# Searching the next batch's bound inside the present batch, and making keys and one-hots during the router

## The reference, cut to what matters

```python
sim = einsum('bhnd,bhmd->bnm', Q, K) / (sqrt(d) * H)     # 4 x 512 x 512
k = int(n * 0.3)                                         # 153
threshold = top_k(sim, k)[0][:, :, -1:]
A = sigmoid(sim) * (sim >= threshold)
A = (A + swapaxes(A, -1, -2)) * 0.5
x = x + (1 - gamma) * layernorm(x) + gamma * A
h = layernorm(x)
scores = sigmoid(h @ router_w)                           # 4 of 8 groups, then 8 of 32 experts
routed = sum over the 8 experts of weight * (silu(h @ w_gate) * (h @ w_up)) @ w_down
shared = silu(h @ sw_gate) * (h @ sw_up) @ sw_down
x = x + routed + shared
```

## Time and profile before

| | us |
|---|---|
| three executions | 1115.98, 1116.62, 1118.31 |
| median | 1116.62 |
| the profiled execution, its own time | 1117.09 |
| its span (first to last instruction) | 1115.4 |

### The profile page before, as it was taken

How to read it: one execution, slowest core, us unless ns; L and a number is a source line. 1 busy time by engine, 2 the same in 40 slices (tenths; PEclk the granted TensorE clock), 3 DMA queues, 4 the chain that set the end, 5 groups by cost and what they waited for, 6 DMA issues and landing times.

```text
span 1115.4 us, 21197 instructions
## 1 busy us (share of the span) xinstructions
PE 925.1 (83%) x4604; PEld 485.6 (44%) x4605; DVE 586.5 (53%) x1362; ACT 457.3 (41%) x894; POOL 514.2 (46%) x396
## 2 busy tenths in 40 slices
PE   3367775775776799999999999999999999999985
PEld 1143342442432355555445555555454454545542
DVE  5959859768555444344644444444544545454321
ACT  5253243241312244345544444454454545454331
POOL 2026126145154055555554555555456463566543
PEclk8568787887887899999999999999999999999998
DMA  5111030110232567777887777778777788786654
GB/s 178 56 39 50 1 119 7 38 41 1 76 116 83 187 130 170 173 169 166 229 179 179 159 166 185 178 156 179 193 181 168 220 181 248 160 179 112 122 108 72
DMA packets 90269, 149.26 MB, mean 134 GB/s; under 512 B 9648, under 2 KB 46768, under 8 KB 90224
## 3 DMA queue, kind: packets, MB, share of 16 engines
q0 software_dynamic: 33120, 80.64, 37.1%
q1 hardware_dynamic: 57104, 68.13, 18.5%
HBM read 101.55 MB, written 47.20 MB: 133 GB/s over the span
## 4 chain that ended last, share of the span: by engine, by line
PE 47%; issue 8%; DVE 3%; DMA 3%; ACT 3%; DVEq 2%; ACTq 2%; POOL 2%; SPq 0%; POOLq 0%
PE bank L254 40%; PE bank L1396 4%; PE bank L1387 3%; DMA stage_dn<-in_L_ffn_w_down_dram 3%; ACT gu L236 2%; DVEq L1069 2%; ACTq L1069 1%; DVE gu L243 1%; POOL mark_q L408 1%; DVE hid L1303 1%; DVE dn L246 0%; POOL mark_q L405 0%; DVE hT L1312 0%; DVEq L243 0%; ACT silu L1164 0%
## 5 line engine op out<-in xcount | busy, mean ns | idle before, releaser
L254 PE MATMUL bank<-gu,xgT 128*128 x1764 | 408.5, 382 | 13.6 <-issue 9.3
L1115 POOL DMA_INDIRECT out_dram<-y,ids_i x145 | 242.0, 1669 | 286.8 <-DMA out_dram<-y,ids_i 152.7
L254 PEld LDWEIGHTS bank<-gu,xgT 128*128 128x128 f16 x1764 | 173.1, 98 | 196.2 <-issue 25.7
L254 PE MATMUL bank<-dn,hT 128*128 x870 | 212.0, 380 | 15.6 <-issue 15.6
L1103 POOL DMA_INDIRECT xg<-xrows,ids_i x153 | 158.3, 1034 | 75.2 <-issue 40.8
L1303 DVE SCALAR_TENSOR_TENSOR hid<-bank,xg,silu 128x256 f32<-128x256 f32 x146 | 70.4, 482 | 207.3 <-ACT silu L1164 180.3
L1176 ACT CAST hT<-bank 128x256 f16<-128x256 f32 x146 | 53.7, 368 | 226.7 <-PE bank L1387 213.7
L1312 DVE TENSOR_TENSOR hT<-bank,hT 128x256 f16<-128x256 f32 x146 | 61.8, 423 | 153.0 <-ACT hT L1176 147.0
L1183 ACT ACTIVATE y<-bank 128x512 f32<-128x512 f32 x145 | 86.6, 597 | 133.4 <-PE bank L254 124.4
L254 PEld LDWEIGHTS bank<-dn,hT 128*128 128x128 f16 x870 | 84.9, 98 | 90.3 <-issue 23.0
L254 PE MATMUL bank<-xT,gu 128*128 128x512 f16 x384 | 98.0, 421 | 25.4 <-DVE hid L303 25.4
(11 more groups left out here) (210 smaller groups left out, 803.6 us busy)
## 6 DMA issues: line engine op xcount, KB each, us to landing
stage_gu<-in_L_ffn_w_gate_dram SPq DMA_DIRECT2D x32, 512.0 KB
stage_gu<-in_L_ffn_w_up_dram SPq DMA_DIRECT2D x32, 512.0 KB
stage_dn<-in_L_ffn_w_down_dram SPq DMA_DIRECT2D x32, 512.0 KB
x_sb<-in_x_dram SPq DMA_DIRECT2D x4, 1024.0 KB, 6.2
xrows<-adj SPq DMA_DIRECT2D x4, 1024.0 KB, 4.1
out_dram<-acc SPq DMA_DIRECT2D x4, 1024.0 KB, 4.4
xg<-xrows,ids_i POOLq DMA_INDIRECT x153
out_dram<-y,ids_i POOLq DMA_INDIRECT x145
```

Source lines behind the costliest of these rows:

```text
L254: last = nc.tensor.matmul(out_ap, stationary(a, c), moving(w, c), start=(c == 0 and (a, w) == parts[0]), stop=(c == chunks - 1 and (a, w) ...
L1115: g_.indirect_dma_start(out, bass.IndirectOffsetOnAxis(ap=ids_i[:, t:t + 1], axis=0), y[:, t % YS, :], None, compute_op=ALU.add).then_inc( ...
```

## The change

The search of batch b + 1 no longer stands at the head of batch b + 1. `search` is cut into `search_step` and `bound`. Batch 0 has its five steps ahead of the loop, as before with two tiles on each engine. For the later batches VectorE counts one tile and ScalarE three, and the steps stand in the batch before: the first guess between the aggregates and the normalising, step 0 after the normalised rows, step 1 after the one-hots, step 2 in the middle of `routing`, steps 3 and 4 behind it. Keys and `mark_slots` of batch p stand ahead of step 1; `mark_parts` is split: the subtraction stays on GpSimd (`part_parts`, after the low parts of the rows), and the comparison goes to VectorE, between steps 3 and 4. The moments of `sim` come from ScalarE: the sum from the copy out of PSUM, the sum of squares from a Square pass. There are two roots a batch for one. All four products of the shared expert stand in `bound` and `update`. `rank_tokens` comes a batch later on TensorE, `sum_marks` after the gate-and-up pieces 0 and 1, `turn_found` a further step on. The down products use banks 7, 5, 6, 7. In the second block the last batch's keys and first product have moved to the end of the first block, and pieces are interleaved in another order.

```diff
-        TB, SIMB, MISC, DB = (0, 1), (2, 3), 4, 7
+        TB, SIMB, MISC = (0, 1), (2, 3), 4
+        DB = (7, 5, 6, 7)
...
+        RANKB = (MISC,) * (B - 1) + (SIMB[0],)
...
         def s_down(pe, b, i):
             pe.wait_ge(S["s_lo"], SC * (b + 1))
-            if b or i:
-                pe.wait_ge(S["added"], RT * b + i)
+            if i == RT - 1:
+                pe.wait_ge(S["added"], RT * b + 1)
...
+        def mark_parts(dve, b, g):
+            n = RT * b + g
+            dve.wait_ge(S["parts_apart"], n + 1)
+            nc.vector.tensor_scalar(mark_q[:, g, :, :], mark_q[:, g, :, :], 0.0, row_idf[:, n:n + 1], ALU.is_equal, ALU.mult).then_inc(S["marks_q_ready"], 1)
...
@@ GpSimd, a batch
-                        pool.wait_ge(S["keys_ready"], b)
-                        for half in range(2):
-                            for g in range(2 * half, 2 * half + 2):
-                                mark_parts(pool, b - 1, g)
-                            s_low(pool, b - 1, 2 * half)
-                            s_low(pool, b - 1, 2 * half + 1)
+                        for c in range(SC):
+                            s_low(pool, b - 1, c)
...
+                    if b >= 1:
+                        pool.wait_ge(S["keys_ready"], b)
+                        for g in range(RT):
+                            part_parts(pool, b - 1, g)
@@ TensorE, a batch
                     if p >= 0:
                         s_gate_up(pe, p, 2)
+                    if p >= 1:
+                        turn_found(pe, p - 1)
...
                     adjacency_T(b)
+                    if p >= 0:
+                        rank_tokens(pe, p)
                     if b + 1 < B:
                         similarities(b + 1)
                     if p >= 0:
                         s_down(pe, p, 1)
-                        sum_marks(pe, p)
                         s_down(pe, p, 2)
-                        turn_found(pe, p)
                     rows_T(b)
...
                     s_gate_up(pe, b, 0)
-                    s_gate_up(pe, b, 1)
-                    rank_tokens(pe, b)
+                    if b + 1 < B:
+                        s_gate_up(pe, b, 1)
+                        if p >= 0:
+                            sum_marks(pe, p)
+                    else:
+                        sum_marks(pe, p)
+                        s_gate_up(pe, b, 1, (0,))
+                        rank_tokens(pe, b)
+                        s_gate_up(pe, b, 1, (1,))
+                        turn_found(pe, p)
@@ ScalarE, a batch
+                    if p >= 0:
+                        s_high(act, p, 0)
+                        s_high(act, p, 1)
+                        s_silu(act, p, 2)
...
                     if more:
                         similarities(b + 1)
+                        squares(b + 1)
+                        nth += 1
+                        root(nth, slice(1, 3))
+                        counts(b + 1, 0, first)
+                    nth += 1
+                    root(nth, slice(0, 1))
+                    if more:
+                        counts(b + 1, 0, second)
+                        counts(b + 1, 1, first)
+                    for i in range(RT):
+                        transposed_rows(b, i)
+                    if more:
+                        counts(b + 1, 1, second)
+                        counts(b + 1, 2, first)
                     act.wait_ge(S["logits_ready"], b + 1)
...
+                        counts(b + 1, 2, second)
                         sigmoids(b + 1)
+                        if p < 0:
+                            convert_high(act, 1)
+                        counts(b + 1, 3, range(1, RT))
                         s_silu(act, b, 0)
+                        counts(b + 1, 4, range(1, RT))
+                        s_silu(act, b, 1)
@@ VectorE, a batch
+                    bound(b)
...
+                    nth = update(b, nth)
+                    if more:
+                        search_step(b + 1, 0)
                         coefficients(b + 1)
+                    if p >= 0:
+                        s_add(dve, p, 2)
+                        find_keys(dve, ch, p)
+                        s_add(dve, p, 3)
+                        for g in range(RT):
+                            mark_slots(dve, p, g)
+                        if not more:
+                            for g in range(RT):
+                                mark_parts(dve, p, g)
+                    if more:
+                        search_step(b + 1, 1)
                     routing(b)
+                    if more:
+                        search_step(b + 1, 3)
+                        if p >= 0:
+                            for g in range(RT):
+                                mark_parts(dve, p, g)
+                        else:
+                            convert_low(dve, 1)
+                        search_step(b + 1, 4)
+                    else:
+                        s_product(dve, b, 0)
+                        find_keys(dve, ch, b)
```

More of the change, by code:

```diff
@@ L692, in similarities, with squares, counts, transposed_rows @@
                         act.wait_ge(S["sim_ready"], RT * b + i + 1)
[L693 removed]
+                        if b == 0:
+                            nc.scalar.mul(sim[:, i, :], bank[SIMB[i % 2]][:, :], SIM_SCALE).then_inc(S["sim_copied"], 1)
+                        else:
+                            nc.scalar.activation(sim[:, i, :], bank[SIMB[i % 2]][:, :], ACT.Identity, scale=SIM_SCALE,
+                                                 accum_out=s_sum[:, i:i + 1]).then_inc(S["sim_copied"], 1)
+                def squares(b):
+                    act.wait_ge(S["act_counted"], counted(b - 1, STEPS - 1))
+                    for i in range(RT):
+                        act.wait_ge(S["sim_copied"], RT * b + i + 1)
+                        nc.scalar.activation(junk[:, i, :], sim[:, i, :], ACT.Square, accum_out=s_sq[:, i:i + 1]).then_inc(S["squares_ready"], 1)
+                def counts(b, k, tiles):
+                    act.wait_ge(S["mid_ready"], b * (STEPS + 1) + k + 1)
+                    if b >= 1:
+                        act.wait_ge(S["squares_ready"], RT * b)
+                    for i in tiles:
+                        nc.scalar.activation(junk[:, i, :], sim[:, i, :], ACT.Sign, bias=mid[:, i:i + 1], scale=-1.0,
+                                             accum_out=act_cnt[:, i:i + 1]).then_inc(S["act_counted"], 1)
+                def transposed_rows(b, i):
+                    act.wait_ge(S["xnT_ready"], RT * b + i + 1)
+                    act.wait_ge(S["xn_ready"], b + 1)
+                    nc.scalar.copy(xT32[:, i, :, :], bank[TB[i % 2]][:, :].rearrange("p (k t) -> p k t", k=KC)).then_inc(S["xT32_ready"], 1)
+                    nc.scalar.copy(xT16[:, 0, :, columns(b, i)],
+                                   bank[TB[i % 2]][:, :].rearrange("p (k t) -> p k t", k=KC)).then_inc(S["xhi_ready"], 1)
                 def sigmoids(b):
@@ new lines, in search_step @@
+                def search_step(b, k):
+                    tiles = DVE_TILES if b == 0 else 1
+                    own, acts = slice(0, tiles), slice(tiles, RT)
+                    dve.wait_ge(S["mid_ready"], b * (STEPS + 1) + k + 1)
+                    if b >= 1:
+                        dve.wait_ge(S["squares_ready"], RT * b)
+                    for i in range(tiles):
+                        ch.done(v.tensor_scalar(junk[:, i, :], sim[:, i, :], mid[:, i:i + 1], 0.0, ALU.is_ge, ALU.add,
+                                                accum_out=cnt[:, i:i + 1]))
+                    ch.settle()
+                    ch.done(v.scalar_tensor_tensor(dlt[:, own], cnt[:, own], -WANTED, slope[:, own], ALU.add, ALU.mult))
+                    dve.wait_ge(S["act_counted"], counted(b, k))
+                    ch.step(v.scalar_tensor_tensor(dlt[:, acts], act_cnt[:, acts], 2 * WANTED - N, slope[:, acts], ALU.add, ALU.mult))
+                    v.scalar_tensor_tensor(mid[:, :], dlt[:, :], DAMPING[k], mid[:, :], ALU.mult, ALU.add).then_inc(S["mid_ready"], 1)
```

254 lines of the change are left out of this document (118 added, 136 removed).

## The result

The kernel before took 1116.3 us (median of four executions, 1115.94 to 1118.31), the changed one 1104.36 us (1102.87 to 1107.48): a ratio of 0.9893, 95% interval 0.9868 to 0.9918. The forecast was 1101.5 in 1094 to 1110. The profiled execution took 1105.09 us with a span of 1103.0; forecast for the span 1100.3. One execution of all those reported here, of the changed kernel with one bank, took 1423.2 us at a granted clock of 0.64 where the others of it had 0.93, and it is in no ratio and no median.

The account below looks back on a forecast made before the run. VectorE, with TensorE close behind, was taken to bound the 369 us before the tile stage. The last addition 15.1 us earlier gave span 1115.4 - 15.1 = 1100.3, predicted time 1101.5 us, range 1094 to 1110.

Parts of the forecast that it names:

- X of batch 1: Start of the four last counts (L852) in batch 1: claimed at 94.3 us, 14.4 earlier than before.
- X to Y: From four last counts to first addition of the transposed adjacency: 30.2 us for 18.1; last batch 29.3 for 18.0.
- Y to T: First addition of the transposed adjacency to end of normalised rows: 16.0 us for 16.6; last batch 12.8 for 16.4.
- R to X: Start of routing to the four last counts, middle batches: 12.9 us for 29.0, 16.1 won.
- T to R: End of normalised rows to start of routing: 18.6 us for 11.9; last batch 14.0 for 9.9.
- Keys end at 318.0: End of the last batch's keys: 318.0 us for 319.55, leaving 1.5 us of the 14.4 won earlier.
- From there 36.1 to the last addition: Last batch's keys to end of the last addition before the tiles: ending at 354.1 us, 15.1 earlier than 369.2.
- (a): Sign is not in the root's table, so more table loads round the second root: +3.8 us, 1105; chance 0.12.
- (b): TensorE's gate-up 2 behind the four last counts is granted 2.4 GHz: 8 us less, 1093.5; chance 0.11.
- (d): TensorE stays at 1.2 GHz through the whole chain of the front: 20 us more, 1121.5; chance 0.07.
- (c): First tile waits for expert weights or rows, so half of the 13.6 us is lost: 1108; chance 0.11.
- (e): The search misses its eight candidates and falls back to 26 bisections: above 1200 us; chance 0.01.

## Why the prediction was right, and where it was off

The forecast, 1101.5 us and faster, held: 1104.36. By its own steps:

- *X of batch 1 at 94.3*: 93.24. *X of batch 2 at 172.0, of batch 3 at 250.0*: 172.39 and 250.99. The forecast had batches 1 and 2 give back 5.0 of the 14.4 us that batch 0 wins, and the last batch most of the rest; batches 1 and 2 gave back 7.0 of 15.5, and the last batch the other 8.5 and 1.5 more. That the two marks came so close is partly luck: a batch is 79.15 and 78.60 long for 77.7 and some 78, but X of batch 1 was 1.1 early.
- *X to Y 30.2, then 29.3 without mixing*: 30.0, 29.5, 28.75. The reason given, TensorE's chain behind product 0, is shown by the runs with the products moved: without it X to Y is 19.6 to 21.4.
- *Y to T 16.0 and 12.8*: 15.2, 15.2 and 12.6. A Square pass took 0.62 for the 0.71 it was priced at. *R to X 12.9*: 12.8 twice.
- *T to R 18.6, and 14.0 in the last batch*: 21.1, 21.1 and 16.3. This is the main term that was mis-sized, by its contention between VectorE and GpSimd. The one-hots were taken at 5.2 with GpSimd beside them and took 6.92, 6.96 and 7.43; step 1 behind them was taken at 1.25 and took 2.1, beside GpSimd's next instructions. That is the 2.5. The bound given for the one-hots, 4.6 to 6.5, was passed, though the forecast had itself put GpSimd beside them, and the earlier trace rows has two of them at 3.23 beside GpSimd, where two take 2.36 elsewhere in the same trace. The keys were late as well, 5.8 for 3.3, beside GpSimd's low parts of the rows (`L379` 1.13 above; 0.29 in the second block's keys, where GpSimd rests), but the last down product hid that: the addition ended 9.7 behind T for the forecast's 9.6, and of the wait of 3.3 ahead of it 0.8 was left.
- *Keys end at 318.0*: 320.94. The 2.9 are mainly the last batch's T to R (2.3); the rest is small terms.
- *From there 36.1 to the last addition*: 38.3. The block change took 1.1 for 0.2. One-hots and multiplications ended 10.8 behind the first for 7.8, again beside the subtractions. The row lists on TensorE were counted at some 2.3 (19.8 to 22.1), as long as before, and took 4.10, at a granted clock of 0.59 behind 3.50 idle, where it was 1.00 before. The first row is the kernel before, the second the changed one:

```profile
348.23 2.39 PE L1367 MATMUL bank<-onehot,tab 128*128 128x164 f32 x16
344.05 4.10 PE L1459 MATMUL bank<-onehot,tab 128*128 128x164 f32 x16 [3.50 <-ACT tab L363]
```

  Against that, the four down products directly behind ran 10.5 for 13.15: the first was at full clock (granted 1.00), which had been priced at 4.93. The forecast had the slow start behind the stop on the down product, and it fell on the lists ahead of it. So the ids were ready at 349.5 for 342, and the last addition ended at 359.2 for 354.1.
- *The tile stage keeps its 746 us*: 743.8. All runs of the changed front lie between 742.9 and 745.3, those of the old front at 746.2 and 747.1. So 5.1 us of lateness before the tiles became 2.7 in the span, which is luck, since the forecast kept the stage as long as it was. What makes the stage shorter wasn't tested.

Of the rivals, (a) is excluded by the rows above: one load stands ahead of the first root, as forecast, and none by Sign or the second root. The 1113 given there for the higher price of a load does not follow from the terms shown; scaled by the two prices, they give about 1109. (b) did not come, gate-up 2 took 7.72 and 7.40. In (d) TensorE would have stayed slow in gate-up 3; that took 5.34 behind gate-up 2 in batches 1 and 3, in batch 2 the same in two pieces, at a granted clock of 1.00. (c) would have shown as a longer tile stage, and it was shorter; (e) did not come either.

What the forecast did not see is how its gain is shared out. It counted the banks among three causes of 15 us. Alone they shorten everything from A to the last addition by 12.5, the net of the whole change being 10.5. Of the 11.5 by which the change shortens K to Z, putting back one bank costs 5, putting back the multiplication 3.4; the removed product 0 was not tried alone there.

## What to carry to other kernels

When work is taken off the busiest engine, look at which of its instructions release another engine, and keep those early: here the place of two 0.7 us products a batch was worth 24 us, twice what the whole change gained. Before a large reordering, try alone the smallest part that removes a stop on the chain; here four banks for one gave as much as the whole change. And where two engines exclude each other, moving the work shifts who waits; it has to go beside instructions that don't collide, or away.

## What the runs showed of the hardware

- VectorE and GpSimd beside each other, both with inputs in SBUF: four one-hots 6.92 to 7.43 for 4.62; four subtractions on GpSimd 6.00 for 4.15; a VectorE instruction on 16 elements a partition 0.90 to 1.02 for 0.16. A count with one large f32 input stayed at 0.74.
- The fp16 multiplication on 128x512 with one SBUF tensor as input took 0.28 alone (1.14 for four), less than the 0.48 of the same shape in f32. In the second block one took 1.24 beside GpSimd, and the last one, with GpSimd idle, 0.34. So it collides too, with one large input. The section of the Trainium skill named above has VectorE's two-port modes contend with GpSimd as well; these rows agree.
- Sign ran behind the root and the root behind Sign with no table load between (62.17 and 62.89 above). A Square pass on 128x512 took 0.62 (59.58 above).
- TensorE behind a stop: the row lists took 4.10 at a granted clock of 0.59 behind 3.50 idle, for 2.39 at 1.00 where no idle time stood before them; the down products directly behind had 1.00.
